# A dense mixture-of-experts feed-forward stage on Trainium2: order of the runs, of the weight loads and of the stores

## The reference, cut to what matters

```python
x = x + 0.5 * L0_ffn(layernorm(x))      # sparse experts
x = x + L0_attn(layernorm(x))
x = x + 0.5 * L0_ffn(layernorm(x))
x = x + 0.5 * L1_ffn(layernorm(x))      # stage f1, first time
x = x + L1_attn(layernorm(x))
x = x + 0.5 * L1_ffn(layernorm(x))      # stage f1, second time

def L1_ffn(x):                           # E = 8 experts, H = 128, K = 2
    scores = sigmoid(x @ gate_W) * route_scale
    topk_scores, topk_idx = top_k(scores, K)
    topk_w = topk_scores / topk_scores.sum(-1, keepdims=True)
    gate_full = scatter of topk_w to the E experts, 0 elsewhere
    h = gelu(einsum('bsd,edh->bseh', x, W1) + b1)
    y = einsum('bseh,ehd->bsed', h, W2) + b2
    expert_out = einsum('bse,bsed->bsd', gate_full, y)
    shared = gelu(x @ Ws1 + bs1) @ Ws2 + bs2
    return expert_out + shared
```

## Time and profile before

| what | value |
|---|---|
| median of three runs | 3428.24 us |
| profiled execution | 3400.82 us |
| span of its trace | 3398.8 us |
| stage f1, first time | 2121.3 to 2441.6 us of the span |
| stage f1, second time | 3070.7 to 3384.4 us of the span |
| store of the output | from 3384.4 us to the end |
| mean granted TensorE clock over the span | 0.924 of full speed |

### The profile page before, as it was taken

The page is one execution under the profiler, slowest core; times in us unless marked ns, Lnnn a source line. Parts: engine busy times, 40 slices in busy tenths (PEclk is TensorE's granted clock), DMA queues, the critical chain, the costliest instruction groups (busy, mean ns, idle before and its releaser), DMA issues. The chain is left out here.

```text
span 3398.8 us, 56446 instructions
## 1 busy us (share of the span) xinstructions
PE 2905.2 (85%) x20629; PEld 2080.4 (61%) x20629; DVE 1733.6 (51%) x4827; ACT 1579.4 (46%) x2598; POOL 1286.1 (38%) x1215
## 2 busy tenths in 40 slices
PE   3599999958999998555999997899859999998997
PEld 3488888823444443345988886566536666665665
DVE  4711111158888788266111111577656666665665
ACT  1133333239988889121333332233237777783332
POOL 3423333359998888043333332000133343320000
PEclk8699999979999999556999999899879999998999
DMA  7179999822554444451999997100066544631001
GB/s 258 44 231 325 317 320 319 264 63 23 59 77 67 58 63 58 49 178 38 296 321 321 315 319 241 37 0 0 19 95 95 81 70 74 90 45 29 0 0 49
DMA packets 368922, 450.78 MB, mean 133 GB/s; under 512 B 87316, under 2 KB 325671, under 8 KB 363559
## 3 DMA queue, kind: packets, MB, share of 16 engines
q1 hardware_dynamic: 344102, 413.98, 47.3%
q0 software_dynamic: 24576, 33.57, 4.6%
HBM read 380.90 MB, written 66.58 MB: 132 GB/s over the span
## 5 line engine op out<-in xcount | busy, mean ns | idle before, releaser
L1542 ACT ACTIVATE f_h_t<-f_h_ps,f_b_t 128x128 f32<-128x128 f32 x1024 | 319.6, 363 | 662.3 <-PE f_h_ps L1501 662.3
L1908 POOL TENSOR_TENSOR a_dmg_buf<-a_c 128x2048 f32<-128x2048 f32 x128 | 520.0, 4087 | 70.8 <-PE a_dmg_ps L1955 45.8
L1501 PEld LDWEIGHTS f_h_ps<-f_rows_t,f_w 128*128 128x128 f32 x4096 | 482.7, 194 | 9.9 <-issue 3.5
L1501 PE MATMUL f_h_ps<-f_rows_t,f_w 128*128 128x128 f32 x4096 | 483.8, 277 | 2.3 <-DVE f_rows_t L1554 1.2
L1512 PE MATMUL f_y_ps<-f_w,f_h_t 128*128 128x256 f32 x2048 | 462.9, 379 | 0.0
L1470 POOL DMA_INDIRECT acc_rows<-f_y,f_give x128 | 203.1, 1587 | 641.7 <-DMA acc_rows<-f_y,f_give 490.1
L1512 PEld LDWEIGHTS f_y_ps<-f_w,f_h_t 128*128 128x128 f32 x2048 | 379.3, 190 | 46.4
L2240 DVE SCALAR_TENSOR_TENSOR a_bond_buf<-a_a,a_small_rep,a_q_ps 128x512 f32<-128x512 f32 x512 | 346.9, 740 | 38.4 <-PE a_bond_ps L1955 36.7
L420 DVE SCALAR_TENSOR_TENSOR f_acc<-f_y_ps,f_gate,f_acc 128x256 f32<-128x256 f32 x576 | 246.5, 479 | 138.0 <-PE f_y_ps L309 132.5
L860 ACT ACTIVATE a_prob<-a_prob,a_neg_top 128x128 f32<-128x128 f32 (+3 forms) x512 | 274.7, 561 | 60.6 <-POOL a_neg_top L674 60.1
L957 DVE CUSTOM_DVE_ANT_0 a_prob<-a_s_ps,a_factor 128x128 f32<-128x128 f32 (+3 forms) x512 | 235.5, 487 | 105.8 <-PE a_s_ps L751 102.4
(11 more groups left out here) (307 smaller groups left out, 4325.8 us busy)
## 6 DMA issues: line engine op xcount, KB each, us to landing
f_w<-in_L_ffn_w_dram SPq DMA_DIRECT2D x256, 1024.0 KB, 7.6
f_b<-in_L_ffn_b_dram SPq DMA_DIRECT2D x128, 128.0 KB, 9.7
a_skewed<-skew SPq DMA_DIRECT2D x8, 2048.0 KB, 8.5
a_q_s<-parts SPq DMA_DIRECT2D x64, 256.0 KB, 10.8
a_k_s<-parts SPq DMA_DIRECT2D x64, 256.0 KB
parts<-a_parts SPq DMA_DIRECT2D x32, 384.0 KB, 7.8
acc_rows<-x_resid SPq DMA_DIRECT2D x17, 512.0 KB, 4.5
xn_rows<-f_xn SPq DMA_DIRECT2D x16, 512.0 KB, 3.1
```

Of the source, the lines that this page charges most:

```text
L1501: last = nc.tensor.matmul(h_ps[n // HB][:, (n % HB) * P:(n % HB + 1) * P], w1_sb[s][:, c, n * P:(n + 1) * P], rows_t[e % 2][:, c, :], star ...
L1542: nc.scalar.activation(h_t[k][:, n, :], h_ps[n // HB][:, (n % HB) * P:(n % HB + 1) * P], ACT.Gelu, bias=b1_t[:, n, e:e + 1]).then_inc(gelu ...
L1908: nc.gpsimd.tensor_tensor(dmg_buf[n % RING][:, :, :], places(c_sb[h], first_place(dg)), c_sb[h][:, PAD:].unsqueeze(1).broadcast_to([P, DG, ...
```

## The change

In stage f1, both times:

- The nine runs start with the shared expert (`RUN` = 8, 0, 1, ..., 7); the biases are the last unit of a batch and not the first.
- VectorE adds each result straight to the residual in `x_resid`; the factor 0.5 is in the gate weights, in the biases' constant gate and in the first add. `acc` and the closing `x += 0.5 * acc` are gone.
- TensorE's first up of the next batch stands at the end of a batch; likewise ScalarE's gelu. The gates of batch `i` are transposed and copied within batch `i` (after down 2 and after add 2). The logits get a wait for that copy.
- VectorE's list keeps its numbers (statistics after add 1, normalise after add 2, and so on), with add `n` now the add of run `n` and add 9 the biases.
- `w1` comes in two DMAs, one for each half of its rows; the loads have several semaphores and another order; at the head VectorE waits only for batch 0 of `x`.
- In the last stage SyncE stores each batch when VectorE is done with it; `store_phase` is gone.

```diff
+    RUN = (E,) + tuple(range(E))
...
         def _(sp):
-            def load(dst, src, **kind):
-                sp.dma_start(dst, src, **kind).then_inc(loaded, 16)
+            sp.dma_start(w1_sb[:, E, :, :], ws1.rearrange("(c p) h -> p c h", p=P)).then_inc(shared_loaded, 16)
             sp.dma_start(gate_w_sb[:, :, :], gate_w.rearrange("(c p) e -> p c e", p=P)).then_inc(gate_loaded, 16)
-            sp.dma_start(route_sb[:, :], route_scale.partition_broadcast(P)).then_inc(gate_loaded, 16)
-            for e in range(E):
-                load(w1_sb[:, e, :, :], w1[e].rearrange("(c p) h -> p c h", p=P))
...
+            sp.dma_start(b1_sb[:, E:NE], bs1.rearrange("(h o) -> h o", o=1)).then_inc(b1_loaded, 16)
+            sp.dma_start(b1_sb[:, 0:E], b1.rearrange("e h -> h e"), allow_slow_non_contiguous=True
+                         ).then_inc(b1_loaded, 16)
+            for c in range(DC):
+                sp.dma_start(w1_sb[:, 0:E, c, :], w1[:, c * P:(c + 1) * P, :].rearrange("e p h -> p e h")
+                             ).then_inc(up_loaded, 16)
...
+            if out_dram is not None:
+                for i in range(B):
+                    sp.wait_ge(batch_done, i + 1)
+                    sp.dma_start(out_dram[i].rearrange("(j p) d -> p j d", p=P), core.x_batch(i)).then_inc(stored, 16)
+                sp.wait_ge(stored, 16 * B)
...
             norm.pe_transpose(0)
-            pe.wait_ge(gate_loaded, 32)
-            logits(0, 0)
-            turn_gates(0, 0)
-            pe.wait_ge(loaded, LOADED)
+            pe.wait_ge(shared_loaded, 16)
+            up(0, 0, 0)
+            pe.wait_ge(gate_loaded, 16)
+            logits(0, 0, guard=False)
+            pe.wait_ge(up_loaded, 16 * DC)
+            pe.wait_ge(down_loaded, 64)
             with pe.Fori(0, B // 2) as pair:
                 for k in range(2):
                     i = pair * 2 + k
-                    up(i, k, 0)
+                    for n in range(NE):
+                        if n + 1 < NE:
+                            up(i, k, n + 1)
+                        down(i, k, n)
+                        if n == 2:
+                            turn_gates(i, k)
+                        if n in (2, 3):
+                            norm.pe_transpose(i + 1, chunks=(n - 2,))
+                        if n == 4:
+                            logits(i + 1, 1 - k)
                     biases(i, k)
-                    for e in range(NE):
-                        if e + 1 < NE:
-                            up(i, k, e + 1)
-                        down(i, k, e)
-                        if e in (2, 3):
-                            norm.pe_transpose(i + 1, chunks=(e - 2,))
-                        if e == 4:
-                            logits(i + 1, 1 - k)
-                        if e == 6:
-                            turn_gates(i + 1, 1 - k)
+                    up(i + 1, 1 - k, 0)
...
                 for k in range(2):
                     i = pair * 2 + k
-                    for e in range(NE):
-                        gelu(i, k, e)
-                        if e == 1:
+                    for n in range(1, NE):
+                        gelu(i, k, n)
+                        if n == 1:
                             norm.act_std(i + 1)
-                        if e == 5:
+                        if n == 5:
                             sigmoid(i + 1)
+                    gelu(i + 1, 1 - k, 0)
...
-                    if n == 0:
-                        last = nc.vector.tensor_copy(acc[:, 2 * half:2 * half + 2, :], y[:, :, :])
+                    if n in (0, NE):
+                        x_half = core.x[:, bass.ds((i + 1) * TPB + 2 * half, 2), :]
+                        last = nc.vector.scalar_tensor_tensor(out=x_half, in0=y[:, :, :], scalar=0.5 if n == 0 else 1.0,
+                                                              in1=x_half, op0=ALU.mult, op1=ALU.add)
                     else:
                         for j in range(2):
                             t = 2 * half + j
+                            x_tile = core.tile(i + 1, t)
                             last = nc.vector.scalar_tensor_tensor(
-                                out=acc[:, t, :], in0=y[:, j, :], scalar=gate[k][:, t, n - 1:n],
-                                in1=acc[:, t, :], op0=ALU.mult, op1=ALU.add)
+                                out=x_tile, in0=y[:, j, :], scalar=gate[k][:, t, RUN[n]:RUN[n] + 1],
+                                in1=x_tile, op0=ALU.mult, op1=ALU.add)
...
-            for i in range(B):
-                core.wait_x(dve, i)
+            core.wait_x(dve, 0)
             norm.dve_stats(0)
...
                         if n == 1:
                             norm.dve_stats(i + 1)
                         if n == 2:
+                            copy_gates(i, k)
                             norm.dve_normalise(i + 1)
                         if n in (3, 4):
                             norm.dve_copy_t(i + 1, 1 - k, chunks=(n - 3,))
                         if n == 5:
                             gates(i + 1, 1 - k)
-                        if n == 7:
-                            copy_gates(i + 1, 1 - k)
-                    nc.vector.drain()
-                    nc.vector.scalar_tensor_tensor(out=core.x_batch(i), in0=acc[:, :, :], scalar=0.5,
-                                                   in1=core.x_batch(i), op0=ALU.mult, op1=ALU.add)
+                    nc.vector.drain().then_inc(batch_done, 1)
```

More of the change, by code:

```diff
@@ L99, in _ @@
                                     fill=1.0, base=0, pattern=[[-1, P]], channel_multiplier=1)
[L102 to L112, removed]
 class Norm:
@@ L245, in ffn1_phase @@
         y_free = sem("y_free")
+        batch_done = sem("batch_done")
+        stored = sem("stored")
         block = ctx.enter_context(nc.Block())
@@ L269, in _ @@
             for k in range(2):
-                last = nc.gpsimd.memset(gate[k][:, :, E:NE], 1.0)
+                last = nc.gpsimd.memset(gate[k][:, :, E:NE], 0.5)
             last.then_inc(const_ready, 1)
@@ L274, in _, with logits @@
         def _(pe):
-            def logits(i, k):
+            def logits(i, k, guard=True):
                 norm.wait_xn_t(pe, i)
+                if guard:
+                    pe.wait_ge(gate_t_copied, i)
                 for j in range(TPB):
@@ L289, in turn_gates, with up, down @@
                 last.then_inc(gate_t_ready, 1)
[L291 to L294, removed]
+            def up(i, k, n):
+                pe.wait_ge(act_ready, i * NE + n + 1)
+                if n == 0:
                     norm.wait_xn_t(pe, i)
                 for c in range(DC):
-                    last = nc.tensor.matmul(h_ps[(k * NE + e) % 2][:, :], w1_sb[:, e, c, :],
+                    last = nc.tensor.matmul(h_ps[(k * NE + n) % 2][:, :], w1_sb[:, RUN[n], c, :],
                                             norm.xn_t[k][:, c, :], start=c == 0, stop=c == DC - 1)
                 last.then_inc(h_ready, 1)
-            def down(i, k, e):
-                pe.wait_ge(act_ready, 2 + i * NE + e + 1)
-                h = h_t[(k * NE + e) % 2]
+            def down(i, k, n):
+                pe.wait_ge(act_ready, 2 + i * NE + n + 1)
+                h = h_t[(k * NE + n) % 2]
                 for half in range(2):
-                    m = 2 * (e + 1) + half
+                    m = 2 * n + half
                     pe.wait_ge(y_free, i * UNITS + m + 1)
@@ L309, in down @@
                         last = nc.tensor.matmul(y_ps[m % YB][:, j, :], h[:, t * P:(t + 1) * P],
-                                                w2_sb[:, e, :], start=True, stop=True)
-                        if e == NE - 1 and t == 0:
+                                                w2_sb[:, RUN[n], :], start=True, stop=True)
+                        if n == NE - 1 and t == 0:
                             last.then_inc(norm.free, 1)
@@ L317, in biases @@
                 for half in range(2):
-                    pe.wait_ge(y_free, i * UNITS + half + 1)
+                    m = 2 * NE + half
+                    pe.wait_ge(y_free, i * UNITS + m + 1)
                     for j in range(2):
                         t = 2 * half + j
-                        last = nc.tensor.matmul(y_ps[half][:, j, :], gate_t[k][:, t * P:(t + 1) * P],
+                        last = nc.tensor.matmul(y_ps[m % YB][:, j, :], gate_t[k][:, t * P:(t + 1) * P],
                                                 b2_sb[:, :], start=True, stop=True)
@@ L351, in sigmoid, with gelu @@
                                      ACT.Sigmoid).then_inc(sig_ready, 1)
[L353 to L358, removed]
+            def gelu(i, k, n):
+                act.wait_ge(h_ready, i * NE + n + 1)
+                nc.scalar.activation(h_t[(k * NE + n) % 2][:, :], h_ps[(k * NE + n) % 2][:, :], ACT.Gelu,
+                                     bias=b1_sb[:, RUN[n]:RUN[n] + 1]).then_inc(act_ready, 1)
             act.sem_inc(act_ready, 2)
             norm.act_std(0)
```

(16 more changed lines are left out.)

26 lines of the change are left out of this document (13 added, 13 removed).

## The result

The changed kernel takes 3625.68 us (median of four runs, 3622.49 to 3630.09), the kernel before 3422.61 us by now (four runs, 3416.62 to 3428.94). The ratio is 1.0594, with a 95% interval of 1.0565 to 1.0622: 203 us slower. The profiled execution spans 3620.4 us, against 3398.8.

The account below looks back on a forecast made before the run. It took stage f1 to be bound by TensorE's list, busy 36.47 of 36.60 us a batch. Heads and ends -26, waits +159 and clock +53 gave +186 on 3428, so 3614 us, range 3535 to 3690.

Parts of the forecast that it names:

- Calls one run later: Stage f1: TensorE waits before down 2, first transposes, second transposes and logits, 9.9 us a batch, 159 in 16.
- The rival in which only the first wait is real: Stage f1: the wait before down 2 alone counts, the other three drown in it; 3483 us, chance 0.05.
- The clock: Stage f1: TensorE returns at lower clock behind the two long waits, 1.65 us each, 3.3 a batch, 53 in 16.
- the two of 1.8 with nothing: Waits before the second transposes and the logits, 1.8 us each: no loss of clock charged behind them.
- the two long waits: TensorE's waits before down 2 (3.74 us) and the first transposes (2.9), each charged 1.65 us of clock.
- The other rival, all four waits with a spell of their own: Stage f1: all four waits cost clock, 6.6 us a batch, 106 in all; 3667 us, chance 0.13.
- The first rival, no clock at all: Stage f1: the four waits come without any loss of clock; 3561 us, chance 0.16.
- Sums straight into x: VectorE's adds in f1: cost taken as 0, upper bound 1.6 us a batch, 26 in all, for computed addresses.
- Heads: Before each pass's loop: up 1 comes 12.7 us earlier in the first pass, 5.7 in the second.
- The loads still cover this: Heads: weight loads land in time for the earlier up 1; if late, they take back at most 5.7 and some 10.
- Ends: Behind each pass's last batch: some 2.3 us lost in the first, about 10 gained at the second's store.
- The sum: Whole kernel: heads and ends -26, waits +159, clock +53, altogether +186 us; forecast 3614 us, chance 0.62.

Follow-up runs that it names:

- experiment 2: The changed kernel with only VectorE's statistics for the next batch moved back, after add 0: 3533.05 us, 1.0335 of the kernel before.
- experiment 3: The changed kernel with statistics after add 0 and normalise after add 1, copies and gates still late: 3483.88 us, 1.0178 of the kernel before.
- experiment 1: The changed kernel with VectorE's calls for the next batch put one add earlier, behind the same downs as before: 3384.82 us, 0.9888 of the kernel before.

## Why the prediction was right

It said 3614 us, in a range of 3535 to 3690, which is +186 us on a median of 3428; measured are 3626, or +203, and 1.059 where 1.054 was forecast.

- **Calls one run later.** Right in its place, sign and size. Forecast 3.44 + 2.9 + 1.8 + 1.8 = 9.9 us in a batch; with the clock held up by fills it is 10.1. With the calls back in place, the loss is gone; with the calls late in the kernel before, it appears. The rival in which only the first wait is real is out by experiment 2: without the first wait the other three still cost 112 us against the kernel before.
- **The clock.** The mechanism was right, the size off: forecast 3.3 us in a batch, measured 4.6. The step that failed is the term "the two of 1.8 with nothing". Each of the two long waits has its stretch at 0.60 and 0.66 of full clock, but behind the two short ones there is one too (0.76 and 0.74), and experiment 3 shows it without the long ones. It is no rule: in 8 of 14 windows of experiment 2 nothing follows the same two short waits. No run has one short wait without the other, so what decides stays open. The other rival, all four waits with a spell of their own (6.6 us), was too high, as 9 of 14 windows of the changed kernel have a clock of 0.90, that of the three stretches above; four have 0.87 or 0.84 and one 0.96. The first rival, no clock at all (3561), is what the kernel with four fills does (3557).
- The Trainium skill's rule (TensorE: Matmul & The Clock Gate, section "HAM oscillation"), that each turn of a loop pays anew for the return to full clock, agrees with the slow stretches in every batch. Its example has them behind waits for loads of some 3 to 5 us; here they stand behind other engines' work, and behind waits of 3.58, 2.32 and, not in every batch, 1.57 us.
- **Sums straight into x.** Forecast 0: an add's median is 476 ns in both kernels, and the batch of experiment 1 is 36.5 us, 0.1 below the kernel before.
- **Heads.** Forecast 12.7 us in the first pass (its own terms give 12.9, as 2129.3 + 3.44 + 3.55 is 2136.3 and not 2136.5), measured 11.7, and that is partly luck. "The loads still cover this" was wrong there: TensorE waits 2.66 us for the last load, as two issues of `w1` take 4.10 us and not 1. What hides most of it is that the logits took 1.85 us and not the 3.55 of the forecast. Forecast 5.7 in the second, measured 7.7: the logits ran at full clock in part (up 0 to up 1 in 5.4 us, not 7.0), and the two issues took 1.34.
- **Ends.** Forecast 10 for the store, measured 11.1 at the end of the span. Forecast a loss of 2.3 at the end of the first pass, measured 2.0, from the last sum to the next stage.
- **The sum.** Heads and ends were forecast to bring 26 us; in the version with the calls back they bring 34 to 36 (3424.02 - 3390.46, 3420.51 - 3384.82), some 2 of it from the shorter batches. By the two profiled executions batches cost 16 x 14.6 = 234 us; heads 11.7 + 7.7 and the end 11.1 come back, 31 in all. That leaves 203, where the forecast had 212 - 26 = 186. That it meets the medians' difference to the microsecond is chance: the same two traces give 113.7 + 108.1 - 11.1 = 211 from the starts and ends of the stages, in part because some batches are longer (53.0 and 52.8 us) and the first pass ends 2 us later behind its last sum. The term that was too small is the clock's, by 1.3 us in a batch or 21 in all.

## What to carry to other kernels

When an engine's list places work by the number of another engine's step ("after add 3"), a change of that numbering moves the work, even where not one of those lines is in the diff. Follow each such call to the run that it now stands behind, and compare the chain behind it with the slack in the trace: here 7.18 us against 6.88 left none, on an engine that was only 70% busy. And price a wait of TensorE with the slow stretch that may follow it: 4.6 of 14.7 us here were not waiting.

## What was not expected of the hardware

Behind two waits of 1.6 us, 5.7 us apart, the granted clock was lower in the changed kernel (0.76 and 0.74), while one gap of 1.9 us alone had left it at 1.00. But the same two waits left it at 1.00 too in most batches of experiment 2, so the distance and length of the waits alone do not decide it. And matmuls whose results nobody reads shortened the kernel: four fills, 22 added passes of 0.43 us or 9.5 us of work in a batch, placed in waits, took 4.6 us off it, since the clock stayed at 1.00 (3557 instead of 3626 us). It is a measure of the waits, not a cure: the same place without the waits gives 3385.
